# Where the softmax of a gated cross-attention is divided: the spread reciprocals on TensorE taken out, the numerators scaled on ScalarE before they are split

## The reference, cut to what matters

```
q = layernorm(x) @ W_q;  k = context @ W_k;  v = context @ W_v
sim  = einsum(q, k) * 64 ** -0.5, masked
attn = softmax(sim)                      # over the 750 keys
out  = einsum(attn, v) @ W_o + b_o
x = x + tanh(g_xattn) * out
...
h = gelu(bitlinear(layernorm(x), w1, b1))
x = x + tanh(g_ffn) * bitlinear(h, w2, b2)
```

## Time and profile before

| what | us |
|---|---|
| median of 3 runs | 1072.77 (1072.48 to 1073.2) |
| the profiled execution | 1070.9 |
| its span, first to last instruction | 1069.1 |
| TensorE busy in it (matmuls) | 995.9 |
| VectorE busy | 835.2 |
| ScalarE busy | 805.7 |
| GpSimd busy | 712.1 |

### The profile page before, as it was taken

The page is one execution under the profiler, slowest core; times in us unless marked ns, Lnnn a source line. Parts: engine busy times, 40 slices in busy tenths (PEclk is TensorE's granted clock), DMA queues, the critical chain, the costliest instruction groups (busy, mean ns, idle before and its releaser), DMA issues. The chain is left out here.

```text
span 1069.1 us, 26540 instructions
## 1 busy us (share of the span) xinstructions
PE 995.9 (93%) x9856; PEld 579.5 (54%) x9856; DVE 835.2 (78%) x1707; ACT 805.7 (75%) x1374; POOL 712.1 (67%) x691
## 2 busy tenths in 40 slices
PE   3988899999999999999999998999999999999877
PEld 2455565565555655555556555556565565555443
DVE  4788798778798777777779876788878776886976
ACT  3976787977878668796868867697786977777766
POOL 5577998577676776567576575767668666956651
PEclk9999999999999999999999999999999999999989
DMA  7989999787879979697877986988867889868750
GB/s 225 280 163 228 206 170 174 133 184 128 163 142 180 174 116 192 115 167 162 157 129 126 200 163 130 183 143 139 177 128 158 175 162 171 167 110 139 148 96 30
DMA packets 472335, 169.17 MB, mean 158 GB/s; under 512 B 450320, under 2 KB 452368, under 8 KB 471824
## 3 DMA queue, kind: packets, MB, share of 16 engines
q1 hardware_dynamic: 472208, 167.48, 80.5%
HBM read 48.28 MB, written 7.34 MB: 52 GB/s over the span
## 5 line engine op out<-in xcount | busy, mean ns | idle before, releaser
L1339 POOL TENSOR_TENSOR p<-prob,p 128x750 f16<-128x750 f32 x224 | 358.5, 1614 | 110.4 <-ACT p L1189 108.1
L1007 DVE CUSTOM_DVE_ANT_0 prob<-ps_s,mbias 128x750 f32<-128x750 f32 x224 | 204.0, 933 | 58.8 <-PE ps_s L820 47.1
L1182 ACT ACTIVATE prob<-prob,rmin 128x750 f32<-128x750 f32 x224 | 204.3, 914 | 26.2 <-DVE rmin L1007 25.8
L787 PE MATMUL ps_g<-ctx,wk 128*128 128x375 f16 x1152 | 201.8, 327 | 23.4 <-POOL ctx L1350 16.4
L787 PE MATMUL ps_g<-wv,ctx 128*128 128x512 f16 (+1 forms) x864 | 197.0, 379 | 4.1 <-DVE k_sb L1026 2.2
L787 PEld LDWEIGHTS ps_g<-ctx,wk 128*128 128x128 f16 x1152 | 111.2, 99 | 105.6 <-issue 25.7
L820 PE MATMUL ps_s<-k_sb,q_sb 64*32 64x375 f16 (+2 forms) x2688 | 128.8, 322 | 15.6 <-DVE rmin L1007 15.4
L787 PEld LDWEIGHTS ps_g<-wv,ctx 128*128 128x128 f16 (+1 forms) x864 | 86.8, 103 | 101.0 <-issue 5.9
L849 PE MATMUL ps_g<-pt,v_sb 128*64 128x224 f16 (+2 forms) x2448 | 122.8, 254 | 2.6 <-DMA pt<-p 2.4
L1189 ACT ACTIVATE p<-prob 128x750 f16<-128x750 f32 x144 | 116.0, 820 | 3.5 <-DMA pt<-p 3.0
L849 PEld LDWEIGHTS ps_g<-pt,v_sb 128*64 128x64 f16 x2448 | 109.6, 110 | 2.9 <-issue 2.8
(11 more groups left out here) (134 smaller groups left out, 1524.6 us busy)
## 6 DMA issues: line engine op xcount, KB each, us to landing
ctx_f<-in_ctx SPq DMA_DIRECT2D x47, 375.0 KB, 4.0
xa<-in_x SPq DMA_DIRECT2D x16, 448.0 KB, 4.7
xr<-in_x SPq DMA_DIRECT2D x28, 256.0 KB, 3.4
out<-xr SPq DMA_DIRECT2D x28, 256.0 KB, 2.8
pt<-p SPq DMA_TRANSPOSE x254, 4.0
h_sb<-in_w SPq DMA_DIRECT2D x4, 512.0 KB, 4.6
w<-in_w SPq DMA_DIRECT2D x3, 512.0 KB, 5.0
xr<-in_w SPq DMA_DIRECT2D x3, 512.0 KB, 5.4
```

The costliest lines, as they stand in the source:

```text
L787: mm = nc.tensor.matmul(out, lhs, rhs, start=(m == 0), stop=(m == len(steps) - 1))
L1007: nc.vector.tensor_tensor_reduce(prob[:, (b * NU + n) % PROBS, :].rearrange("p (c k) -> p c k", c=2), ps_s[:, n % 2, :, 0:CH], mbias[:, :] ...
L1182: nc.scalar.activation(prob[:, (b * NU + n) % PROBS, :], prob[:, (b * NU + n) % PROBS, :], ACT.Exp, bias=rmin[:, n:n + 1], scale=-1.0, acc ...
L1339: nc.gpsimd.tensor_tensor(p16[:, u % HILO, 1, 0:J], prob[:, (b * NU + n) % PROBS, :], p16[:, u % HILO, 0, 0:J], ALU.subtract).then_inc(s[" ...
```

## The change

The numerators are divided before they are split, and nothing is spread or divided behind the weighing.

- **R** is taken for the two units of one m, 7 times in a batch instead of 4: one reciprocal of [128 x 2], then two multiplications by 512 of [128 x 1], in place. It waits for the second E of its pair.
- **N**, new, on ScalarE: the unit is multiplied by its reciprocals in place in `prob` (float32), for the 12 units of a batch other than 4 and 11.
- **H** for those 12 is a copy on GpSimd, behind N; **L** for them stays a subtraction on GpSimd.
- For units 4 and 11, H is one scaling copy on ScalarE from `prob` to float16, and L is one `scalar_tensor_tensor` on VectorE (times the reciprocal, minus the high part).
- The 40 spreading matmuls of a batch, the copy of the spread reciprocals and the multiplication are gone. **PL** on ScalarE makes the high part of the attention from PSUM, and **PA** on VectorE the low part from PSUM; GpSimd has no PL, and `att` and `rrec16` are gone. The bank is freed by that low part.
- One wait is added: ahead of the first write of `xc` for the first tile (L2 with t = 0), VectorE waits for all 16 items WA of ScalarE, which use the same memory. In VectorE's list, WS:1:0, which has that same wait, is the next item.
- All five lists are written anew with these items. In the lists of a middle batch PV:0 stands some five items later behind S:5 than before (then it came next or next but one).

```diff
-    "O": ("x2", 1), "V": ("v_lo", 1), "F1": ("h_lin", NF), "PV": ("attn_raw", 1), "Q": ("q_lo", 1),
+    "O": ("x2", 1), "V": ("v_lo", 1), "F1": ("h_lin", NF), "PV": ("attn_lo", 2), "Q": ("q_lo", 1),
...
-HI_ON_ACT = [n for n in range(NU) if n not in (2, 5, 7, 10, 12)]
-HI_ON_POOL = [n for n in range(NU) if n not in HI_ON_ACT]
+LO_ON_DVE = (4, 11)
+LO_ON_POOL = [n for n in range(NU) if n not in LO_ON_DVE]
...
                 elif kind == "PV":
-                    need(pe, "recips", b, recips_for(b, n))
-                    j, first_query, size, row = weighs(b, n)
-                    for m in units_of(b, n):
...
-                                    nc.tensor.matmul(g[e * DH:(e + 1) * DH, to:to + many],
-                                                     rrec16[:, a, u:u + 1].to_broadcast([128, DH]),
-                                                     ident[:, at:at + many], start=(a == 0), stop=(a == 1))
+                    j, _, size, row = weighs(b, n)
...
+            def take_reciprocals(b, m):
+
+                need(dve, "expd", b, 2 * m + 1)
+                need_lo(dve, b - 1, 2 * m + 1)
+                nc.vector.reciprocal(rrec[:, 2 * m:2 * m + 2], rsum[:, 2 * m:2 * m + 2]).then_inc(s["recips_raw"], 1)
+                need(dve, "recips_raw", b, m)
+                for u in (2 * m, 2 * m + 1):
+                    nc.vector.tensor_scalar(rrec[:, u:u + 1], rrec[:, u:u + 1], RS, None, ALU.mult)\
+                        .then_inc(s["recips"], 1)
...
-                    need(dve, "p_lo", b, n - PROBS)
+                    need_lo(dve, b, n - PROBS)
...
+                elif kind == "L" and n in LO_ON_DVE:
+                    u = b * NU + n
+                    dve.wait_ge(hi_act, b * len(LO_ON_DVE) + LO_ON_DVE.index(n) + 1)
+                    nc.vector.scalar_tensor_tensor(out=p16[:, u % HILO, 1, 0:J], in0=prob[:, u % PROBS, :],
+                                                   scalar=rrec[:, n:n + 1], in1=p16[:, u % HILO, 0, 0:J],
+                                                   op0=ALU.mult, op1=ALU.subtract).then_inc(lo_dve, 1)
                 elif kind == "PA":
-                    need(dve, "recips_out", b, n)
-                    qs = slice(0, queries_of(b, n))
-                    nc.vector.tensor_tensor(att[:, qs], g[:, qs], att[:, qs], ALU.mult)\
-                        .then_inc(s["attn_raw"], 1)
+                    pieces = attn_pieces(b, n)
+                    need(dve, "attn_hi", b, 2 * n + 1)
+                    for at, to, size in pieces:
+                        nc.vector.scalar_tensor_tensor(out=attn[:, 1, n % NP, to:to + size], in0=g[:, at:at + size],
+                                                       scalar=1.0 / RS, in1=attn[:, 0, n % NP, to:to + size],
+                                                       op0=ALU.mult, op1=ALU.subtract)\
+                            .then_inc(s["attn_lo"], 2 // len(pieces))
...
+                    if t == 0:
+                        dve.wait_ge(w_abs, 2 * NW)
...
+                elif kind == "N":
+                    held = prob[:, (b * NU + n) % PROBS, :]
+                    need(act, "recips", b, n)
+                    nc.scalar.activation(held, held, ACT.Copy, scale=rrec[:, n:n + 1]).then_inc(normed, 1)
...
-                elif kind == "PV":
-                    need(act, "weighted", b, n)
-                    need(act, "attn_lo", b, 2 * n - 1)
-                    nc.scalar.activation(att[:, 0:queries_of(b, n)], g[:, 256:256 + queries_of(b, n)], ACT.Copy, scale=1.0 / RS)\
-                        .then_inc(s["recips_out"], 1)
...
-                if kind == "H" and n in HI_ON_POOL:
+                if kind == "H" and n in LO_ON_POOL:
 
                     u = b * NU + n
-                    need(pool, "expd", b, n)
+                    pool.wait_ge(normed, b * len(LO_ON_POOL) + LO_ON_POOL.index(n) + 1)
                     need_turned(pool, u - HILO)
```

More of the change, by code:

```diff
@@ L287 @@
+    F2:1:15
 """)
 POOL_SEQ = in_order("""
[L289 to L292 removed]
@@ L439, in turns_before @@
     return sum(len(turned_parts(v // NU, v % NU // 2)) for v in range(u % HILO, u + 1, HILO))
-def recips_units(b, n):
-    return slice(2 * n, 2 * n + 2) if b == LB else slice(4 * n, min(4 * n + 4, NU))
-def recips_for(b, n):
-    last = 2 * units_of(b, n)[-1] + 1
-    return last // 2 if b == LB else last // 4
 def emptied(kind, n, b):
@@ L460, in emptied @@
         return name, tile_of(b, n // times) * times + n % times + 1
-    return name, b * PER_BATCH[name] + n + 1
-HI_ON_ACT = [n for n in range(NU) if n not in (2, 5, 7, 10, 12)]
-HI_ON_POOL = [n for n in range(NU) if n not in HI_ON_ACT]
+    return name, b * PER_BATCH[name] + times * (n + 1)
+LO_ON_DVE = (4, 11)
+LO_ON_POOL = [n for n in range(NU) if n not in LO_ON_DVE]
 def build(nc, x_d, ctx_d, mask_d, gx_d, gf_d, wq_d, wk_d, wv_d, wo_d, bo_d, w1_d, b1_d, w2_d, b2_d, out_d):
@@ L825, in emit @@
                 elif kind == "PV":
-                    need(pe, "recips", b, recips_for(b, n))
-                    j, first_query, size, row = weighs(b, n)
-                    for m in units_of(b, n):
-                        for of, q, at, many in pieces_of(b, m):
-                            if of != j or not first_query <= q < first_query + size:
-                                continue
-                            to = 256 + q - first_query
-                            for a in range(2):
-                                for e in range(2):
-                                    u = 2 * m + e
-                                    nc.tensor.matmul(g[e * DH:(e + 1) * DH, to:to + many],
-                                                     rrec16[:, a, u:u + 1].to_broadcast([128, DH]),
-                                                     ident[:, at:at + many], start=(a == 0), stop=(a == 1))
+                    j, _, size, row = weighs(b, n)
                     for m in units_of(b, n):
@@ L1177, in emit @@
                 p = b % 2
-                g = bank(kind, n, b) if kind in EMPTIED else None
+                filled = {"PL": "PV"}.get(kind, kind)
+                g = bank(filled, n, b) if filled in EMPTIED else None
                 if kind == "E":
@@ L1200, in emit @@
                     for at, to, size in pieces:
-                        nc.scalar.activation(attn[:, 0, n % NP, to:to + size], att[:, at:at + size], ACT.Copy)\
-                            .then_inc(s["attn_hi"], 2 // len(pieces))
+                        nc.scalar.activation(attn[:, 0, n % NP, to:to + size], g[:, at:at + size], ACT.Copy,
+                                             scale=1.0 / RS).then_inc(s["attn_hi"], 2 // len(pieces))
                 elif kind == "K":
@@ L1328, in emit @@
                 p = b % 2
[L1329 removed]
+                if kind == "H" and n in LO_ON_POOL:
                     u = b * NU + n
[L1332 removed]
+                    pool.wait_ge(normed, b * len(LO_ON_POOL) + LO_ON_POOL.index(n) + 1)
                     need_turned(pool, u - HILO)
[L1334 to L1335 removed]
+                    nc.gpsimd.tensor_copy(p16[:, u % HILO, 0, 0:J], prob[:, u % PROBS, :]).then_inc(hi_pool, 1)
+                elif kind == "L" and n in LO_ON_POOL:
                     u = b * NU + n
[L1338 to L1347 removed]
+                    pool.wait_ge(hi_pool, b * len(LO_ON_POOL) + LO_ON_POOL.index(n) + 1)
+                    nc.gpsimd.tensor_tensor(p16[:, u % HILO, 1, 0:J], prob[:, u % PROBS, :],
+                                            p16[:, u % HILO, 0, 0:J], ALU.subtract).then_inc(lo_pool, 1)
                 elif kind == "CX":
```

541 lines of the change are left out of this document (260 added, 281 removed).

## The result

The changed kernel takes 1043.09 us (median of 4 runs, 1039.71 to 1046.32) where the kernel before takes 1072.62 (1072.18 to 1073.2) beside it: a ratio of 0.9724, 95% interval 0.9684 to 0.9764. It is 29.5 us faster. Forecast were 1060, 1046 to 1080.

What follows compares the result with a forecast made beforehand. The prediction took TensorE's pace to bound the middle, three quarters of the time. Its terms, -15.4 - 2.4 - 2.7 + 8 = -12.5 us, from a median of 1072.8 gave 1060 us, range 1046 to 1080.

Steps and rivals of the forecast that it cites:

- Price of all this: Middle of the span: fuller ScalarE and VectorE and a longer unit path raise TensorE's 25.8 us idle time; +8 us.
- The spreading, 15.4: TensorE: removing the spreading matmuls saves 15.4 us by start-to-start times; their full busy time, 26.6, is the upper end.
- The waits for reciprocals, 2.4, and the tail, 2.7: TensorE's two waits ahead of the spreading go, 2.4 us; fewer steps between last weighing and projection save 2.7 us.
- ScalarE, +66: ScalarE: 224 scaling copies, 205.2 us, replace copies of 116.0 and 23.0 us; busy time +66, to 872.
- VectorE, +34: VectorE: new multiplications, reciprocals, PA and L against old R and PA; busy time +34, to 869, between +20 and +134.
- GpSimd, -6: GpSimd: 112 more copies +92.8, 32 fewer subtractions -51.6, PL's 46.8 gone; busy time -6 us.
- The path of a unit: After its exponential a unit also waits for its partner, R and N: 2.4 us at least, some 3.2 with one item ahead.
- slots run short: Rival: the five slots are held 3.2 us longer, so VectorE and TensorE wait more; 1078, up to 1094 us; chance 0.22.
- in each other's way: Rival: VectorE and GpSimd contend, VectorE at 969 us, TensorE's middle idle time doubles; 1078, or 1065 to 1072; chance 0.10.
- frees nothing: Rival: the spreading ran while TensorE would have waited for turned numerators anyway; 1078 us; chance 0.05.
- TensorE is not the bound: Rival: the fullest other engine, VectorE with 835 us, is the bound and its +34 stand in full; 1107 us; chance 0.03.
- all 26.6 us come back: Rival: the spreading's full busy time is saved and idle time doesn't grow; 1041 us; chance 0.10 for 1050 and less.

Runs made afterwards that it cites:

- b_exact: Kernel before, full reciprocals and all spreading kept; R's small steps remade as one-element steps, the low part reading a column of scalars: 1055.68 us, ratio 0.9841.
- b_nospread: Kernel before without its 640 spreading matmuls, so the output is not divided rightly; R and lists as before: 1070.18 us, ratio 0.9976.
- b_stt1: Kernel before with R in one-element steps, the low parts made by a step of two SBUF inputs for each unit: 1086.89 us, ratio 1.0135.
- a_wide2: Changed kernel with R's two one-element multiplications made one of two elements, plus 64 unused two-source steps: 1060.31 us, ratio 0.9885.

## Why the prediction was wrong in size, point by point

- **What bounds the kernel.** Right that TensorE's pace sets the middle and that its waits for M are the ones to look at. But the waits of the earlier trace rows were read only as a margin that an addition could use up. I didn't follow them back one step further, to what makes M late; that was R.
- **The step that failed** is "Price of all this: TensorE's 25.8 us of idle time in the middle grows ... I take +8". It fell by 15.5. The bound "between nothing and doubled" had no side on which it falls, though the VectorE paragraph had just shown that R's waits end. Those waits entered the sum only as VectorE's busy time, 85.3 to 65.4, in an engine with 165 us to spare, and so at no gain. In b_exact the busy time hardly changes (833.8 for 835.2) and the time falls by 17 us. What the other additions cost TensorE beside that gain, the part that the +8 was meant for, no run takes apart. With the idle time's -15.5 for +8 the sum would have been 1036.8. The other terms make up the rest: +1.7 for the busy time's 13.7, +2.4 for the two waits, which the 15.5 hold already, +4.7 at the tail (2.0 lost for 2.7 gained), +2.6 at the start, together 1048.2 for a median, or 1046.3 less the 1.9 by which the profiled execution of the kernel before lay under its median; the profiled one of the changed kernel took 1046.32.
- **The spreading, 15.4.** TensorE's busy time fell by 13.7 (the forecast of "near 969" for it took off the whole 26.6; 982.2 came). As time on TensorE's queue the start-to-start reading of the earlier trace rows was good, and the full 26.6 was not. As a gain of the span it was too much: 2.6 us with R's waits in place, 3.5 to 7.3 without. Work taken from the bound brings its full length only where nothing else is late.
- **The waits for reciprocals, 2.4, and the tail, 2.7.** The first are gone. At the tail, the last weighing ends at 1014.09 (11.89 + 2.20 in the rows below) and the projection starts 0.97 us later, as forecast ("about 1.0"):

```profile
1011.89 2.20 PE L831 MATMUL ps_g<-pt,v_sb 128*64 128x128 f16 x72
1014.05 0.42 ACT L1188 ACTIVATE attn<-ps_g 128x128 f16<-128x128 f32 x2
1014.42 0.49 DVE L999 SCALAR_TENSOR_TENSOR attn<-ps_g,attn 128x128 f16<-128x128 f32 x2 [1.65 <-ACT attn L1188]
...
1015.06 1.24 PE L781 MATMUL ps_g<-wo,attn 128*128 128x512 f16 x5
```

  But TensorE's idle time in the last 132 us grew by 2.0 all the same: the 2.7 us were given back within the tail. At the start, 3.1 us were lost to a later first product, which the prediction doesn't have.
- **ScalarE, +66.** N took 913 ns against the 916 forecast. The sum came to +53.5: neighbouring copies overlap, so that the 224 were 170.1 + 29.2 = 199.3 and not 205.2, PL from PSUM is 24.2 where it was 28.0 from SBUF, and other lines lost 3.0. It cost nothing visible: TensorE waited less than before with ScalarE at 667 of 779 us.
- **VectorE, +34.** The mechanism was right and nearly every size too high: one-element multiplications 24.1 for 47.0, PA 26.8 for 30, L 44.1 for 49 (1.379 us each, inside 1.3 to 1.8). That alone gives +2.1; the other 9.7 of the fall to 827.6 are other lines, the split of x for one, 42.0 us before and 31.0 after. By the Trainium skill (SBUF — State Buffer, Who interferes with whom) VectorE and GpSimd exclude each other for a whole instruction where VectorE runs in a mode that uses both port pairs, or reads two tensors from SBUF while GpSimd's instruction reads SBUF. The trace agrees for the steps around 421 us, which end as a GpSimd instruction does; the 8.27 us above are more than one instruction's length, for that step was passed over by eight of them. I had taken that rule only as speaking against the change, for L, where it speaks for it, since the change removes the 67 two-source steps of R from a place with waiters.
- **GpSimd, -6** came to +8.4: the copies added 165.1 - 66.2 = 98.9 and not 92.8 (865 ns each, 829 before), the subtractions took off 358.5 - 308.9 = 49.6 and not 51.6, and other lines added 5.9. Nothing in the span hung on it: GpSimd waited 140.3 us for N.
- **The path of a unit and the slots.** Longer by N and the pair's wait, and covered: VectorE waits 9 times, 7.1 us, for a slot, less than before. The rival "slots run short" did not come, and neither did "in each other's way", "frees nothing" (though b_nospread shows it nearly true for as long as R's waits stand) nor "TensorE is not the bound".
- The rival "all 26.6 us come back" came nearest to the measured time, with 1041 for 1043, by luck: 13.7 came back, and the rest of its gain is idle time, which it left as it was.

## What to carry to other kernels

A short instruction that sometimes takes ten times its shortest time, with the same shape, is a wait to be followed up, and its price is not its share of busy time: ask what is listed behind it and who waits for that. Here 52 us of such waits stood on an engine busy for 78%; with as much steady work in their place the kernel was 17 us faster. Before work is moved off the fullest engine, follow that engine's own waits back two steps; what makes the releaser late may be worth more than the work, and be removed by rewriting one line.

## What the runs showed of the hardware that was not expected

- Single-source steps of [128 x 1], also with a second operand as a column of scalars, never waited for GpSimd: 142 to 160 ns, and 204 to 219 ns with the column, in 224 instructions of each kind in several kernels. At two elements (f32) the mean was 486 ns, at four and two (f16 out) 490, up to 1610. The Trainium skill (VectorE: DVE Perf Modes, What auto-detection actually checks) gives the mode with both port pairs to a single source and a destination in SBUF whose outermost dimensions other than 1 are both even or equal; the 486 ns at two elements and the 149 at one agree with that as far as they go.
- A step of two tensors from SBUF waits even at one element: 56 of 224 over 0.25 us, up to 8.27 us, across eight instructions of GpSimd without a turn for VectorE between them.
- Such a step seldom waited right behind one that had itself just waited, where no semaphore wait lies between: 3 of 49 in b_stt1, against 23 of 108 behind one that hadn't. In a_wide2 one of the 64 added steps waited, and none of the 25 behind a multiplication that had. In the kernel before, where R's second step waits for a semaphore of the first, it waited in 25 of the 39 cases in which the first had.
